# Groups of four transposed score fills in the last two batches, and an earlier place for two pieces of GpSimd work

## What is computed

```python
x = x + tanh(g_xattn) * gamma * attention(layernorm(x), ctx, ctx)
#   per head: softmax((q.T k) / sqrt(16)) over the 256 context positions, times v.T; k and v are ctx
x = x + tanh(g_ffn) * ffn(layernorm(x))
#   ffn: gate = silu((x Wg) * gate_scale); up = (x Wu) * up_scale
#        out  = ((gate * up) Wd) * down_scale      with Wg, Wu: 256 x 768, Wd: 768 x 256
#        all three weights rounded to float8 e4m3 first
```

## Time and profile before

| | |
|---|---|
| median of three runs | 210.3 us |
| the profiled execution | 209.54 us |
| its span, first to last instruction | 207.8 us |
| TensorE matmuls busy | 194.7 us (94%) |
| VectorE busy | 160.8 us (77%) |
| GpSimd busy | 145.9 us (70%) |
| ScalarE busy | 123.3 us (59%) |

### The profile page before, as it was taken

The page is one execution under the profiler, slowest core; times in us unless marked ns, Lnnn a source line. Parts: engine busy times, 40 slices in busy tenths (PEclk is TensorE's granted clock), DMA queues, the critical chain, the costliest instruction groups (busy, mean ns, idle before and its releaser), DMA issues.

```text
span 207.8 us, 4727 instructions
## 1 busy us (share of the span) xinstructions
PE 194.7 (94%) x1785; PEld 118.3 (57%) x1785; DVE 160.8 (77%) x338; ACT 123.3 (59%) x240; POOL 145.9 (70%) x167
## 2 busy tenths in 40 slices
PE   8579999999999999999998999999999998799991
PEld 5225456655665566556564554456667656566581
DVE  3699989999999987698977893325967666464985
ACT  2014668776867687677767368955448442864450
POOL 5994889957999999992799503395365998276440
PEclk9969999999999999999999999999999999999998
DMA  6799601101122231131221222311320003003033
GB/s 192 214 353 388 145 2 54 31 26 50 54 90 71 57 128 34 55 120 60 91 94 52 82 78 56 105 55 55 110 101 2 0 3 101 0 0 104 0 103 101
DMA packets 19783, 17.75 MB, mean 85 GB/s; under 512 B 4016, under 2 KB 19248, under 8 KB 19760
## 3 DMA queue, kind: packets, MB, share of 16 engines
q1 hardware_dynamic: 19760, 17.44, 26.8%
HBM read 11.02 MB, written 6.42 MB: 84 GB/s over the span
## 4 chain that ended last, share of the span: by engine, by line
PE 71%; DVE 11%; POOL 10%; ACT 3%; issue 3%; DMA 1%; SPq 0%; DVEq 0%; POOLq 0%; ACTq 0%
PE ps L777 19%; PE ps L818 15%; PE ps L851 13%; PE ps L789 10%; DVE neg_max L573 6%; PE ps L923 6%; PE ps L792 4%; POOL f_lo L430 4%; PE ps L805 2%; PE ps L802 1%; ACT xn L510 1%; POOL x_sb L393 1%; POOL p_t L440 1%; POOL u_n L390 1%; DMA c_sb<-in_ctx 1%
## 5 line engine op out<-in xcount | busy, mean ns | idle before, releaser
L573 DVE TENSOR_REDUCE neg_max<-ps 128x2 f32<-128x512 f32 x128 | 79.4, 681 | 11.0 <-PE ps L777 10.8
L777 PE MATMUL ps<-km,qn 32*128 32x512 f32 x256 | 71.4, 639 | 4.5 <-POOL qn L357 3.7
L481 ACT ACTIVATE p_t<-ps 128x512 f32<-128x512 f32 x128 | 66.6, 600 | 15.1 <-PE ps L792 13.3
L789 PE MATMUL ps<-qm,c_sb 32*128 32x512 f32 x256 | 70.8, 631 | 0.3 <-DVE neg_max L573 0.3
L430 POOL TENSOR_TENSOR f_lo<-fu,f_hi 128x512 fp32r<-128x512 f32 x23 | 29.3, 1277 | 27.2 <-ACT f_hi L499 27.2
L851 PE MATMUL ps<-w_exp,w_gu 128*128 128x512 f16 x192 | 45.4, 380 | 1.0 <-DVE fu L691 1.0
L792 PE MATMUL ps<-max_t,sel 4*128 4x256 bf16 x256 | 33.7, 268 | 0.0
L818 PE MATMUL ps<-p_t,v_t 128*32 128x256 f32 x512 | 30.9, 382 | 0.0
L685 DVE SCALAR_TENSOR_TENSOR ga<-th,ps 128x512 f32<-128x512 f32 x24 | 16.4, 682 | 18.7 <-ACT th L494 18.7
L792 PEld LDWEIGHTS ps<-max_t,sel 4*128 4x128 bf16 x256 | 18.0, 94 | 21.6 <-issue 18.6
L777 PEld LDWEIGHTS ps<-km,qn 32*128 32x128 f32 x256 | 24.5, 187 | 9.5 <-issue 9.1
(11 more groups left out here) (70 smaller groups left out, 227.3 us busy)
## 6 DMA issues: line engine op xcount, KB each, us to landing
u_scr<-u_sb SPq DMA_DIRECT2D x32, 128.0 KB
u_n<-u_scr SPq DMA_DIRECT2D x16, 128.0 KB
r_n<-r_scr SPq DMA_DIRECT2D x16, 128.0 KB
out_x<-p_t SPq DMA_DIRECT2D x16, 128.0 KB, 1.9
x_sb<-in_x SPq DMA_DIRECT2D x3, 512.0 KB, 7.6
c_sb<-in_ctx SPq DMA_DIRECT2D x3, 512.0 KB, 8.5
w_all<-in_L_ffn_gate_w SPq DMA_DIRECT2D x1, 768.0 KB, 9.2
w_all<-in_L_ffn_up_w SPq DMA_DIRECT2D x1, 768.0 KB, 9.8
```

What stands on the lines that cost most here:

```text
L481: nc.scalar.activation(p_t[:, b % 2, i, :], ps[:, bank_of["t", n][0], :], ACT.Exp, scale=DH ** -0.5).then_inc(exp_ok, 1)
L573: nc.vector.tensor_reduce(neg_max[:, b % 2, at:at + PAR, 0], ps[:, bank_of["s", n][0], :].rearrange("p (e l) -> p e l", e=PAR), axis=AX.X, ...
L777: nc.tensor.matmul(ps[:, bank, :], qn[rows, b % 2, P * t:P * (t + 1)], km[rows, b % 2].rearrange("p e l -> p (e l)"), start=True, stop=Tru ...
L789: nc.tensor.matmul(ps[:, bank, :], c_sb[rows, b, P * t:P * (t + 1)], qm[rows, b % 4].rearrange("p e l -> p (e l)"), start=True, stop=False)
```

## The change

The first edit moves three `t` fills, each to the group before its own. TensorE's order becomes: s127, t112 to t115, P13, T15, t116 to t119, G0, t120 to t123, G1, t124 to t127, P14, G2, P15, G3. ScalarE's exponentials follow in the same groups. Banks change with the order. The other two edits change where GpSimd does `result` and `rstd_chunk(3)`. Nothing is added or left out.

```diff
-LAST_STEPS = "tttPTttttGttttGtttttQGR"
+LAST_STEPS = "ttttPTttttGttttGttttQGR"
 ...
-                    if c == 2 and it == 1:
+                    if c == 2 and it == 0:
                         rstd_chunk(3)
-                    if it == 4 and 0 < c < NCH - 1:
+                    if it == 2 and 0 < c < NCH - 1:
                         result(c - 1)
 ...
-            for i in range(3):
+            for i in range(4):
                 exps(NB - 2, i)
             max_out(NB - 1)
             v_out(NB - 1)
-            for i in range(3, 7):
+            for i in range(4, FILLS):
                 exps(NB - 2, i)
             act.wait_ge(coef_ok, 2)
             gate_tanh(0, 0)
-            exps(NB - 2, 7)
-            for i in range(3):
+            for i in range(4):
                 exps(NB - 1, i)
             gate_tanh(1, 1)
             fused_high(0, 0)
-            for i in range(3, FILLS):
+            for i in range(4, FILLS):
                 exps(NB - 1, i)
 ...
             scores(FILLS * NB - 1)
-            for i in range(3):
+            for i in range(4):
                 scores_t(n + i)
             weighted(NB - 3)
             turn(NB - 1)
-            for i in range(3, 7):
+            for i in range(4, 8):
                 scores_t(n + i)
             gate_up(0, 0)
-            for i in range(7, 11):
+            for i in range(8, 12):
                 scores_t(n + i)
             gate_up(0, 1)
-            for i in range(11, 2 * FILLS):
+            for i in range(12, 16):
                 scores_t(n + i)
             weighted(NB - 2)
             gate_up(0, 2)
```

## The result

The changed kernel takes **208.87 us** (median of 18 runs, 208.0 to 210.38) against 210.29 us for the kernel before (18 runs, 209.5 to 211.8). The ratio is **0.9925**, 95% interval 0.9901 to 0.9949: faster, by less than 1%. The forecast was 208.8 us, within 1%.

A forecast was written before the change was run, and what follows sets the result against it. From 125 us the chain of waits was taken to run along TensorE except in one stretch. Fills -0.80 and GpSimd moves -0.74 make -1.54 us: 210.3 to 208.8 us, forecast 208.4 to 209.2, range 207.9 to 210.3.

The forecast's parts named there:

- The lone fill before P14: TensorE, end of attention: groups of four shrink the last group from 2.35 to 1.31 us, -1.04 us.
- t115 before P13: TensorE, end of attention: t115 now precedes P13 and waits for its bank, delaying P13 by 0.24 us (bounds 0 to 1.17).
- result(0) before low(9), low(10) 1.88 later: GpSimd, feed-forward chunk 2: the earlier addition makes low(10) 1.88 us late, down(10) 170.24, gate_up(16) 176.84, 0.99 later.
- stall of 1.8 us: TensorE, chunk 2: a new stall of 1.8 us at down(10), which waits for low(10).
- The power, 1.69 sooner: GpSimd's power moved behind low(12): ScalarE's norm_apply(3) starts at 175.10, 1.69 us earlier.
- gate_up(17) and gate_up(18): TensorE, end of chunk 2: gate_up(17) at 180.41, 0.60 us earlier; gate_up(18) at 183.09, -0.74 us.
- The handover from VectorE to TensorE: Chunk 2: fu(14) at 176.03 releases gate_up(16) 0.81 us later, at 176.84; then TensorE runs without stall to gate_up(17).
- result(1), no cost: GpSimd: result(1) moves behind low(14), delaying low(15) to 182, before down(15) needs it at 184.6; no cost.
- Rival 1: Second place: low(10)'s lateness is not paid back by the power; 211.4 us if all kept, 210.5 if part; chance 0.10.
- Rival 2: First place: t115 starts only with t114's last matmuls, delaying P13 by about 1.1; 209.6 us; chance 0.07.
- Rival 3: Second place breaks even: VectorE's order takes 0.7 us more than counted, only the first edit gains; 209.5 us; chance 0.13.
- Rival 4: Both terms at their best: t115 hidden and gate_up(18) a full 1.0 us sooner; 208.3 us; chance 0.15.

The follow-up runs named there:

- t115 by itself: Kernel before with only t115 moved in front of P13 (groups of four, three, four, five), lone fill before P14 kept: 210.54 us, ratio 1.0.
- the two kernels not in the table: Changed kernel with result back behind low(10): 208.63 us, ratio 0.989; changed kernel with result one step sooner, behind low(7) and low(13): 206.82 us, ratio 0.9824.

## Why the prediction was right, point by point

- **The lone fill before P14, -1.04.** Right. The last group takes 1.31 us as the full group of before did, and the two experiments with the fills leave -1.02.
- **t115 before P13, +0.24.** Right in kind, 0.1 too small: P13 is 0.34 late in the changed kernel, and `gate_up(3)` 0.32 with t115 by itself. The start was right and the length was not. These are the weight loads of the lone fill before and of t115 now:

```profile
131.09 0.29 PEld L789 LDWEIGHTS ps<-qm,c_sb 32*128 32x128 f32 x2
121.30 0.29 PEld L788 LDWEIGHTS ps<-qm,c_sb 32*128 32x128 f32 x2
```

And these are the passes around each: count, then the shortest, the median and the longest in ns:

```profile
L789 PE MATMUL ps<-qm,c_sb x6: 586/587/589, 130.5 to 131.6; 32*128 32x512 f32 x6
L788 PE MATMUL ps<-qm,c_sb x7: 587/587/692, 120.8 to 121.8; 32*128 32x512 f32 x7
```

t115's load and first pass start together at 121.30, which is 120.48 on the clock of before, just where I had put it (120.44 and 0.04 for the semaphore). From there to P13 it takes 1.27, not the lone fill's 1.17. The lone fill's weights began to load 0.10 ahead of its first pass at 131.19, and that pass took 0.59; t115 is the one pass of 0.69. I took the price of a fill whose weights were already on their way for one that had to wait for its bank.

- **result(0) before low(9), low(10) 1.88 later.** The step was right: `low(10)` at 168.99, `down(10)` at 170.31. Reduced to the clock of before by the 0.12 that TensorE stands later from P14 on (132.48 against 132.36), that is 168.87 and 170.19 (forecast 168.91 and 170.24), and `gate_up(16)` is at 176.79 (176.84). The "stall of 1.8 us" is that lateness; the idle time in the row is 1.54.
- **The power, 1.69 sooner.** `norm_apply(3)` at 175.17, reduced 175.05 (forecast 175.10).
- **gate_up(17) and gate_up(18).** 180.48 and 183.16, reduced 180.36 and 183.04 (forecast 180.41 and 183.09). The handover from VectorE to TensorE came where it was put, by a narrow margin. `gate_up(16)` at 176.91 stands 0.80 behind its `fu(14)`, which is the forecast's 0.81:

```profile
176.11 0.75 DVE L690 SCALAR_TENSOR_TENSOR fu<-ps,gus,ga 128x512 f32<-128x512 f32 x1
```

It also stands 2.78 behind `gate_up(15)` at 174.13, and an undisturbed unit takes 2.69, so TensorE would have been there 0.1 us sooner. The view shows no wait that short, and the chain of waits shows TensorE alone from `down(10)` on.

- **result(1), no cost.** Right: `low(15)` starts at 181.97 (forecast 182), TensorE shows no stall behind `down(10)` up to the end, and the last interval is the same to 0.1.
- **Rival 1, the lateness stays.** The nearest test is the experiment with the addition alone. There it is real, but smaller than the 1.88 that I had put for all of it: 1.22. Even kept with the first edit it would have given +0.5, not a slower kernel by 1%. The power pays it back, as argued.
- **Rival 2**, program order, needed P13 to be 1.1 late; it is 0.34. **Rival 3** needed nothing to be gained at the second place; it is -0.78. **Rival 4** needed t115 for nothing and -1.0 at the second place.

The two places missed in opposite directions: the first edit gave 0.1 less than forecast (-0.70 for -0.80) and the other two 0.04 more (-0.78 for -0.74). That the sum comes as close as -1.49 for -1.54 is in part luck. The forecast also held that a measurement of this kernel can't tell 1% from no change; with 18 runs on each side the interval is 0.24% to either side, and 0.75% is clear of it.

What the prediction did not do is price the two GpSimd edits apart. It had `gate_up(16)` 0.99 later from the one and `norm_apply(3)` 1.69 sooner from the other, but summed them into one term of -0.74 at `gate_up(18)`. By the experiments it is -1.64 from the power and +0.86 from the addition beside it. The replay had the steps for both; the same replay for each edit by itself would have pointed to the better kernel.

## What to carry to other kernels

Price each edit of a change by itself, also where they meet on one engine: a sum that is small and negative can hide one edit that gains twice as much and one that costs half of it. When work that nobody waits for must stand in an in-order queue, put it where that engine already waits for an input (here 2.04 us in front of `low(8)`, for an addition of 2.3 us), not in a row with work that others wait for. And where the executions of a kernel scatter by more than the effect, compare the intervals between landmarks of two traces rather than their spans.

## What the runs showed of the hardware

The executions fall into groups by TensorE's granted clock in the first 20 us. In the profiled executions where it was 0.91 (before, fills only, power only), `turn(14)` starts at 117.54, 117.63 and 117.47; where it was 0.80 or 0.81 (changed, both moves, addition alone, fills and power, t115 alone), between 118.24 and 118.39; and at 117.94 in the one where it was 0.78, so the mean alone doesn't order them. From 18 to 21 us the first three had 1.00 (2.4 GHz) and the other six 0.50 (1.2 GHz). The work up to there is the same in all. That is some 0.8 us between executions of the same instructions, as much as either part of this change. No run varies the clock by itself, so that the clock is the cause is argued, not shown.

Executions with about the same mean granted clock can be compared by their times. These are all of those whose clock was recorded and whose mean over the whole execution was 0.984 to 0.992; the two kernels not in the table have none.

| kernel | executions | us | mean less before's | by the landmarks |
|---|---|---|---|---|
| before | 8 | 209.41 to 209.62 | | |
| changed | 5 | 208.0 to 208.17 | -1.4 | -1.49 |
| fills only | 5 | 208.77 to 208.96 | -0.6 | -0.72 |
| both GpSimd moves only | 1 | 208.88 | -0.6 | -0.79 |
| result only | 1 | 210.74 | +1.2 | +1.22 |
| power only | 3 | 207.83 to 207.92 | -1.6 | -1.64 |
| t115 only | 5 | 209.91 to 210.07 | +0.5 | +0.31 |

Behind the start-up the executions repeat: 43 to 47 us of four engines handing work to each other agree to 0.02 us from one execution to another: 45.90, 45.88 and 45.89 in the three kernels that share the GpSimd order of before, 45.12 twice with both moves, and 44.26 and 44.27 with the power alone.

A fill that has its row group free does not start behind the small matmuls of the fill before it: in the changed kernel t115's first pass starts at 121.30, and the small matmuls of the two fills ahead of it start only at 121.71 and 121.92. t115 cost 0.32 to 0.34 us, not 1.1. "TensorE: Matmul & The Clock Gate" in the Trainium skill, Part 3, has matmuls start and end strictly in program order; the order of starts here does not agree. Four fills took 1.31 us, against 1.17 for one whose weights began to load 0.10 ahead and 1.27 for one whose did not. The prediction's 3.6 compares with the first; with the second it is 4 x 1.27 / 1.31 = 3.9.
